# A graph layer and a mixture of experts on one core: two sort products cut in three, and a third output buffer in the last stage

## The reference

```python
def layernorm(x): return (x - mean(x)) / sqrt(var(x) + 1e-5)

# x (6250, 256); src, dst, edge_weight (100000,)
h   = layernorm(x) @ gnn_W.T
x   = x + segment_sum(edge_weight[:, None] * h[dst], src, 6250)

z   = layernorm(x)
top, which = top_k(z @ gate_w + gate_b, 2)          # of 16 experts
share      = softmax(top)
moe = sum over the two of share * (relu(z @ w1[e] + b1[e]) @ w2[e] + b2[e])
y   = z + moe
out = x + layernorm(y) * gamma + beta
```

## Time and profile before

| | us |
|---|---|
| median of three executions (2127.3 to 2132.4) | 2129.42 |
| the profiled execution | 2131.93 |
| its span, from the first to the last instruction | 2129.9 |
| VectorE busy | 978.4 |
| GpSimd busy | 1276.2 |
| TensorE matmuls busy | 1480.1 |

### The profile page before, as it was taken

The page is one execution under the profiler, slowest core; times in us unless marked ns, Lnnn a source line. Parts: engine busy times, 40 slices in busy tenths (PEclk is TensorE's granted clock), DMA queues, the critical chain, the costliest instruction groups (busy, mean ns, idle before and its releaser), DMA issues. The chain is left out here.

```text
span 2129.9 us, 33319 instructions
## 1 busy us (share of the span) xinstructions
PE 1480.1 (69%) x7822; PEld 1164.8 (55%) x7823; DVE 978.4 (46%) x2239; ACT 507.8 (24%) x1490; POOL 1276.2 (60%) x1156
## 2 busy tenths in 40 slices
PE   6007888057767677777777777776169999989563
PEld 4007887034545454554454545554159989978552
DVE  8999999033333332323333333233743333323265
ACT  4542111000101010101010101010635444434363
POOL 1003999757777777777777777777025545544423
PEclk9559999557887887878788888788589999999886
DMA  5111000023333333333333333334542232263363
GB/s 169 35 35 54 3 2 2 14 86 105 104 104 103 103 104 104 104 105 103 104 103 104 103 104 103 103 103 101 137 153 71 70 106 70 89 190 111 102 209 111
DMA packets 107264, 201.62 MB, mean 95 GB/s; under 512 B 19940, under 2 KB 68699, under 8 KB 107096
## 3 DMA queue, kind: packets, MB, share of 16 engines
q0 software_dynamic: 52672, 139.93, 22.6%
q1 hardware_dynamic: 43352, 46.50, 6.7%
q10 hardware_dynamic: 11200, 14.68, 2.2%
HBM read 165.17 MB, written 35.86 MB: 94 GB/s over the span
## 5 line engine op out<-in xcount | busy, mean ns | idle before, releaser
L805 POOL DMA_INDIRECT hbuf<-xn_rows,ix x832 | 798.3, 960 | 273.0 <-issue 237.4
L848 PE MATMUL bank<-hbuf,picks 128*128 x2032 | 661.0, 466 | 275.0 <-SPq L793 274.2
L848 PEld LDWEIGHTS bank<-hbuf,picks 128*128 128x128 f32 x2032 | 418.2, 225 | 498.1 <-issue 443.5
L831 DVE TENSOR_SCALAR picks<-iota_two,marks 128x256 f32<-128x256 f32 x832 | 332.5, 442 | 701.7 <-PE bank L848 686.3
L376 POOL DMA_INDIRECT edge_groups<-work,dest_i x56 | 215.7, 3853 | 201.2 <-DVE work L584 184.7
L719 PE MATMUL bank<-work 128*128 128x192 bf16 x1568 | 146.7, 251 | 130.3 <-DVE work L577 130.3
L1312 PEld LDWEIGHTS bank<-rowsT,w_sb 128*128 128x128 f32 x1744 | 212.3, 193 | 28.9 <-issue 24.2
L1312 PE MATMUL bank<-rowsT,w_sb 128*128 128x128 f32 x1744 | 215.6, 277 | 17.9 <-issue 17.9
L914 ACT ACTIVATE agg<-bank 128x256 f32<-128x256 f32 x49 | 18.8, 383 | 870.8 <-PE bank L848 870.8
L1254 POOL DMA_INDIRECT expert_out<-y_sb,to_i x112 | 111.1, 992 | 168.9 <-DVE y_sb L1356 159.0
L719 PEld LDWEIGHTS bank<-work 128*128 128x128 bf16 x1568 | 135.1, 98 | 135.3 <-issue 134.7
(11 more groups left out here) (247 smaller groups left out, 1323.3 us busy)
## 6 DMA issues: line engine op xcount, KB each, us to landing
w_sb<-in_L_ffn_w_dram ACTq DMA_DIRECT2D x28, 512.0 KB, 5.0
hbuf<-xn_rows,ix POOLq DMA_INDIRECT x832, 2.8
xn_rows<-xn SPq DMA_DIRECT2D x11, 896.0 KB, 4.0
ya<-expert_out SPq DMA_DIRECT2D x7, 896.0 KB, 5.9
yb<-expert_out SPq DMA_DIRECT2D x7, 896.0 KB, 7.9
x<-in_x_dram SPq DMA_DIRECT2D x6, 896.0 KB, 11.1
out_dram<-o SPq DMA_DIRECT2D x7, 512.0 KB, 2.9
xn_rows<-x SPq DMA_DIRECT2D x3, 896.0 KB, 4.0
```

The lines of the kernel that those rows point to most:

```text
L805: pool.indirect_dma_start(hbuf[:, 1 + j, k, :], None, xn_dram, bass.IndirectOffsetOnAxis(ap=ix[:, 2 * j + k:2 * j + k + 1], axis=0)).then_ ...
L831: s = v.tensor_scalar(picks[:, j % 2, k, :], iota_two[:], marks[:, 0, 2 * j + k:2 * j + k + 1], marks[:, 1, 2 * j + k:2 * j + k + 1], ALU. ...
L848: m = nc.tensor.matmul(bk[q][:, 0:D], picks[:, j, k, q * P:(q + 1) * P], hbuf[:, ds(place + j, 1), k, :].rearrange("p s d -> p (s d)"), st ...
```

## The change

There are two parts.

**In the sort**, the products L564 and L577 of VectorE are each issued as three instructions, over three, two and two of the seven pairs of edge columns. The semaphore is raised by the third. What is computed stays the same, and the small one-hot table (L568) stays one instruction.

**In the last stage**, `o` has three buffers in place of two, and VectorE waits at the head of group t for the output of group t - 3. The factors of group t stand ahead of `scale` of group t - 1. The first loads are cut: three windows of `ya` and `yb` first, on a semaphore of their own, then the other four.

```diff
+                SHORT = [(0, 3), (3, 5), (5, HB)]
                 def hots(n):
...
-                    v.tensor_tensor(rowhot[n % RP], iota_rows[:, None, :, :].to_broadcast([P, HB, 2 * P, 2]),
-                                    row_b[:, c, ts].rearrange("p (h b) -> p h b", b=2)[:, :, None, :].to_broadcast([P, HB, 2 * P, 2]), ALU.is_equal).then_inc(rowhot_ready, 1)
+                    for h0, h1 in SHORT:
+                        s = v.tensor_tensor(rowhot[n % RP][:, h0:h1, :, :], iota_rows[:, None, :, :].to_broadcast([P, h1 - h0, 2 * P, 2]),
+                                            row_b[:, c, ts].rearrange("p (h b) -> p h b", b=2)[:, h0:h1, None, :].to_broadcast([P, h1 - h0, 2 * P, 2]), ALU.is_equal)
+                    s.then_inc(rowhot_ready, 1)
...
-                    v.tensor_tensor(fields[n % RM], colhot[n % RJ][:, :, None, :, :].to_broadcast([P, HB, VALUES, SP_, 2]),
-                                    pieces[:, pairs, :, None, :].to_broadcast([P, HB, VALUES, SP_, 2]),
-                                    ALU.mult).then_inc(fields_ready, 1)
+                    for h0, h1 in SHORT:
+                        s = v.tensor_tensor(fields[n % RM][:, h0:h1, :, :, :], colhot[n % RJ][:, h0:h1, None, :, :].to_broadcast([P, h1 - h0, VALUES, SP_, 2]),
+                                            pieces[:, pairs, :, None, :][:, h0:h1].to_broadcast([P, h1 - h0, VALUES, SP_, 2]), ALU.mult)
+                    s.then_inc(fields_ready, 1)
...
-        o = [sb(f"o{q}", [P, WB, D], fp32) for q in range(2)]
+        RO = 3
+        o = [sb(f"o{q}", [P, WB, D], fp32) for q in range(RO)]
...
-                load(0)
+                for to, k in ((ya[0], 0), (yb[0], 1)):
+                    sp.dma_start(to[:, 0:EARLY, :], y_dram[k * NP:EARLY * P + k * NP, :].rearrange("(w p) d -> p w d", p=P)).then_inc(early_in, 16)
+                for to, k, there in ((ya[0], 0, ya_in[0]), (yb[0], 1, yb_in[0])):
+                    sp.dma_start(to[:, EARLY:WB, :], y_dram[EARLY * P + k * NP:WB * P + k * NP, :].rearrange("(w p) d -> p w d", p=P)).then_inc(there, 16)
                 load(1)
...
-                    pe.wait_ge(ya_in[q], 16 * (t // 2 + 1))
-                    pe.wait_ge(yb_in[q], 16 * (t // 2 + 1))
                     for j in range(WB):
                         w = t * WB + j
+                        if w == 0:
+                            pe.wait_ge(early_in, 32)
+                        elif j == 0 or w == EARLY:
+                            pe.wait_ge(ya_in[q], 16 * (t // 2 + 1))
+                            pe.wait_ge(yb_in[q], 16 * (t // 2 + 1))
...
-                    if t >= 2:
-                        dve.wait_ge(out_sent[t % 2], 32 * (t // 2))
+                    if t >= RO:
+                        dve.wait_ge(out_sent[t % RO], 32 * (t // RO))
...
                     s.then_inc(mv3_ready, 1)
-                    if t > 0:
-                        scale(t - 1)
                     dve.wait_ge(std3_ready, t + 1)
                     link(v.reciprocal(rs3[:], std3[:]))
                     link(v.scalar_tensor_tensor(sh3[:], mv3[:, :, 0], -1.0, rs3[:], ALU.mult, ALU.mult))
                     dve.sem_inc(norm3_ready, 1)
+                    if t > 0:
+                        scale(t - 1)
```

More of the change, by code:

```diff
@@ L1383, in gnn_moe_kernel @@
         sh3 = sb("sh3", [P, WB], fp32)
+        assert (WT - 1) % RO == 0
         HALVES = [(0, WB // 2 + 1), (WB // 2 + 1, WB // 2)]
         LATE = 2
+        EARLY = 3
+        early_in = sem("early_in")
         ya_in = [sem(f"ya_in{q}") for q in range(2)]
@@ L1399, in gnn_moe_kernel @@
         out_ready = sem("out_ready")
-        out_sent = [sem(f"out_sent{q}") for q in range(2)]
+        out_sent = [sem(f"out_sent{q}") for q in range(RO)]
         last_own = sem("last_own")
@@ L1423, in _ @@
                         sp.dma_start(out[(t * WB + w) * P:(t * WB + w + n) * P, :].rearrange("(w p) d -> p w d", p=P),
-                                     o[t % 2][:, w:w + n, :]).then_inc(out_sent[t % 2], 16)
+                                     o[t % RO][:, w:w + n, :]).then_inc(out_sent[t % RO], 16)
                 w0 = (WT - 1) * WB
@@ L1430, in _ @@
                 sp.dma_start(out[(NW - 1) * P:N, :], o[0][0:LASTW, WB - 1, :]).then_inc(out_sent[0], 16)
-                sp.wait_ge(out_sent[0], 32 * ((WT - 1) // 2) + 48)
-                sp.wait_ge(out_sent[1], 32 * (WT // 2))
+                sp.wait_ge(out_sent[0], 32 * ((WT - 1) // RO) + 48)
+                for q in range(1, RO):
+                    sp.wait_ge(out_sent[q], 32 * (WT // RO))
             @block.tensor
@@ L1459, in _ @@
                 for t in range(WT):
-                    q = t % 2
+                    q = t % RO
                     if t + 1 < WT:
@@ L1472, in _ @@
                     for k, (w, n) in enumerate(HALVES):
-                        here = o[t % 2][:, w:w + n, :]
+                        here = o[t % RO][:, w:w + n, :]
                         pool.wait_ge(scaled, t * 2 + (k + 1))
@@ L1494, in stats @@
                     dve.wait_ge(o_added, t * WB + j + 1)
-                    return v.bn_stats(stats3[:, j, :], o[t % 2][:, j, :])
+                    return v.bn_stats(stats3[:, j, :], o[t % RO][:, j, :])
                 for t in range(WT):
-                    if t >= 2:
-                        dve.wait_ge(out_sent[t % 2], 32 * (t // 2))
+                    if t >= RO:
+                        dve.wait_ge(out_sent[t % RO], 32 * (t // RO))
                     dve.sem_inc(dve_steps, 1)
@@ L1503, in _ @@
                         dve.wait_ge(y_summed, w + 1)
-                        v.tensor_tensor(o[t % 2][:, j, :], summed(w), xn2[:, w, :], ALU.add).then_inc(o_added, 1)
+                        v.tensor_tensor(o[t % RO][:, j, :], summed(w), xn2[:, w, :], ALU.add).then_inc(o_added, 1)
                         if j > 0:
```

## The result

| | before | changed |
|---|---|---|
| median of four executions each, us | 2128.94 | 2117.31 |
| lowest to highest, us | 2127.3 to 2132.4 | 2116.65 to 2117.97 |
| span of the profiled execution, us | 2129.9 | 2115.5 |
| GpSimd's last scatter of the sort starts at | 422.54 | 437.60 |
| last stage, first load issued to the end of the span, us | 114.9 | 85.3 |

The ratio of the times is 0.9944, with a 95% interval of 0.9929 to 0.9959: by the ratio 11.9 us faster, between 8.7 and 15.1 (the medians lie 11.6 us apart). The forecast was 2076.3 with a range of 2066 to 2098, so it was wrong by 41 us. Rival 1 had said 2117.5.

The account below looks back on a forecast made before the run. It took GpSimd's scatter tail in the sort and the wait for the store in the last stage as bounds. -25.5 - 28.9 = -54.4 us gave 2077.5 or 2075.0, middle 2076.3; own range 2066 to 2088, 8 in 10 2066 to 2098.

Parts of the forecast that it names:

- Rival 1: Sort: shorter pieces don't let GpSimd in, the tail stays and 15.7 us are paid; -13.2 in all, 2117.5 us; chance 0.14.
- The tail is on the path and is worth its length: Sort: 38 scatters between 376 and 424 us hold up the next stage; predicted gain -25.5 us, the cut's cost included.
- the passage between two products: Sort: where one VectorE product gives way to the next, GpSimd's scatter gets in if asking under 0.79 to 1.14 us.
- The walk round the batch: Sort: from each passage the next comes after 0.2 to 0.7 us, 0.87 at worst, so a scatter costs under 2 us.
- The cost of the cut: Sort: four more VectorE instructions per batch, 224 at 0.07 us, cost 15.7 us, with bounds of 0 and 34.
- (a): Last stage, start: the first matmul waits for three of seven windows, not a whole group; -2.9 us, bounds -3.5 and -1.
- (b): Last stage, third buffer: cycles of 8.4 us set by ScalarE, the second 10.2; 43.8 us against 71.3, so -27.5 us.
- (c): Last stage, end: GpSimd's late residual add and late last stores cost +1.5 us, between -1 and +4.
- The sum of the last stage: Last stage: its three terms, -2.9 - 27.5 + 1.5, give -28.9 us.
- Rival 3: Shared port decides in both places: Rival 1 in the sort, last-stage adds wait out GpSimd's; +10.6, 2141 us; chance 0.03.

Follow-up runs that it names:

- r_take: The last stage alone plus a reciprocal of seven float32 elements once per chunk, ahead of the two reductions: 2060.11 us, ratio 0.9678.
- gap7: The last stage alone plus a reciprocal of seven float32 elements behind the small one-hot table in each of the 56 batches: 2064.19 us, ratio 0.9692.
- r_moved: The last stage alone, no added instruction, with the layer norm's last-group factors (holding a reciprocal) issued four batches later: 2102.87 us.
- sort_only: The kernel before with only the cut of the sort's two products into three instructions each: 2144.2 us against 2129.44, ratio 1.007.
- tt7: The last stage alone plus, in each batch, a float32 product of seven elements in place of the reciprocal of gap7: 2065.7 us.
- the last stage alone: The changed kernel with the sort's products of before, uncut: 2102.32 us, ratio 0.9872 against the kernel before.
- cut_gap: The changed kernel, products cut in three, plus a reciprocal of seven elements after the small one-hot table in every batch: 2106.96 us.
- r_age: The last stage alone plus a reciprocal once per chunk, alternately four and seven VectorE products ahead of the reductions: 2060.88 us.
- r_twice: The last stage alone plus the reciprocal in batches 20 and 37 of 56 only: 2065.65 us.

## Why the prediction was wrong, point by point

- *The tail is on the path and is worth its length*: right. With all scatters let in (r_take) the kernel gains 2102.32 - 2060.11 = 42.2 us, and the wait for the records falls from 52.7 to 11.7.
- *"GpSimd can take the passage between two products only if it comes soon after it has begun to ask, with the limit between 0.79 and 1.14 us"*: this is the step that failed. It was read from two scatters that got in and two that didn't, and the first two had a cause that the same timeline held: the layer norm's factors, with their reciprocal at 180.76, ahead of the reductions. In gap7 a scatter gets in after 1.14 us and in r_moved one after 1.43 (196.83 + 2.27 - 0.84 = 198.26); in the changed kernel one is kept out after about 0.6. What decides, with whole products, is a state that a reciprocal of seven float32 elements brings about (r_take) and that is lost when GpSimd pauses. Shorter pieces of the same bfloat16 products don't bring it about. The -41.2 us of the tail did not come, and that is the whole miss. The walk round the batch holds where scatters are let in: the first chunk's took 1.06 to 1.51 us.
- *The cost of the cut, 15.7 us at 0.07 each*: 14.8 at 0.066 (sort_only), 15.06 by the last scatter's start. Right.
- *(a) Early loads -2.9*: the first matmul comes 4.50 us after the first load, where it was 8.10, so -3.6, just beyond the bound of -3.5. The first aggregation gains 5.2, since TensorE's pairs of matmuls went from 1.06 to 0.59 us, with the granted clock from 0.50 to 1.00, sooner: 3.2 us behind its start here, 6.1 before (its rows at 2037.92 and 2029.24). The sum had no term for that. A part is given back in the next cycle (+1.1): TensorE is idle for 1.39 us ahead of the second group.
- *(b) Cycles of 8.4 us and one of 10.2, -27.5*: 8.35, 8.23 and 8.36 where nothing is late, 9.19 in place of 10.2, and one of 10.65 where the stores stood ahead of loads on one queue and TensorE's clock fell after its wait. I had the queue only as a bound, for all cycles, and the clock not at all. Together 44.78 against 43.8, -26.7.
- *(c) The end +1.5*: +1.3.
- *The sum of the last stage -28.9*: -29.5 in the profile, -27.1 in timed runs. Right. Rival 3's waiting adds didn't come: 0.41 and 0.42 us each beside GpSimd's.
- *Rival 1 at 0.14*: it came true with its number, 2117.5 against 2117.31. That the pieces wouldn't help, and that the first chunk was an exception for another reason, was the better reading, and I had set against it only that the shapes were the same. Its mechanism held in part: a gapless row of products doesn't keep scatters out by itself, since in r_take all of them pass beside one. That its number fits to 0.2 us is in part luck: the cut cost 0.9 us less and the last stage gave 1.8 less in timed runs than it had put in, and it started from 2130.7 where the median was 2128.94.

In the runs a scatter that is let in ends 0.84 us after the product (gap7), and one that isn't is passed over at the ends of twelve instructions (three in each of four batches) and more. The Trainium skill, "SBUF — State Buffer", section "A bandwidth-pool intuition that's wrong (but worth ruling out)", has such a transfer "blocked until DVE-end + ~115 ns", measured beside a `tensor_copy`. If that meant the end of any one instruction in a row of them, the wait for the records in the kernel before would be about the 11.7 us of r_take, as an estimate; it was 52.7, and the measurement decides. The Trainium skill, same page, section "Who interferes with whom", tells of a probe in which `tensor_tensor` did not stall transfers; the section also says that a `tensor_tensor` with both inputs in SBUF contends with a GpSimd instruction that reads SBUF. Here the gapless bfloat16 products do keep the scatters out. The scatters take their indices from a table in SBUF (`dest_i`), so this may be the second case; no run here tells the two apart. The number of inputs doesn't sort the openers: the float32 product of seven elements has two inputs in SBUF and gives a place (tt7).

**What stays open.** What the state is. Which property of the reciprocal lets later scatters in at the ends of ordinary products, why a float32 product makes only one place, and why cut products undo both after a few chunks. A look at the neighbours' starts and ends gave no difference between a place taken and one missed. No version was tried with an opener other than a reciprocal beside cut products, with pieces of other sizes, or with a bfloat16 instruction of seven elements or a float32 one of 64, which would part width from size.

## What to carry to other kernels

When one engine gets in only sometimes, list every instruction in front of the times that it did, small ones and other stages' too, before making a rule of lengths; and test the rule by making the others fail (r_moved) as well as by making them pass. Where indirect DMAs of GpSimd take as long as several of VectorE's instructions beside gapless bfloat16 products, try one float32 reciprocal of a few elements shortly before GpSimd starts to ask, before cutting the products: here it was worth 42 us on the last stage alone, with whole products, and cutting cost 14.8. A shared queue of loads and stores should be costed at the cycle in which both first meet.

## What the runs showed of the hardware that was not expected

- A scatter of 0.97 us took up to 16.4 us beside VectorE, through four batches of eight instructions each (cut_gap), while with whole products a reciprocal of 0.19 us, once per chunk, keeps all of them under 2 us (r_take).
- With whole products, the state that lets scatters in outlasts idleness of 4.19 us and not of 7.89 us (r_age, r_twice).
- A cut of an instruction in a gapless row costs 0.066 us, less than half the fixed part of 0.15 us that the prediction worked out from the durations.
